# Turning the channel tiles of a Mamba block by transposing DMAs instead of by TensorE

## What is computed

```python
proj = einsum('bsd,ed->bse', xn, in_proj_w)        # gate 8192, hBC 10240, dt 128
gate, hBC, dt = split(proj)
hBC  = silu(causal_conv_of_4_taps(hBC) + conv_b)   # per channel, along the tokens
hs, Bm, Cm = split(hBC)                            # 8192 channels; 8 groups x 128; 8 x 128
dt   = clip(softplus(dt + dt_bias), 0, 100);  A = -exp(A_log)
# chunks of 128 tokens, every head h: A_cum is the running sum of dt*A in the chunk
Y_diag = (Cc @ Bc.T * exp(segsum(dt*A))) @ (hs*dt)
Y_off  = (Cc @ state) * exp(A_cum);  state = state*exp(A_cum[-1]) + Bc.T @ (hs*dt*exp(A_cum[-1]-A_cum))
y   = Y_diag + Y_off + hs*D
g   = y * silu(gate);  g = g * rsqrt(mean(g*g over 1024 channels) + 1e-5) * norm_w
out = x + g @ out_proj_w.T + base_and_lora(xn)
```

## Time and profile before

| | |
|---|---|
| median of the runs | 1740.48 us |
| the profiled execution, its own time | 1741.34 us |
| its span, first to last instruction | 1740.0 us |
| PE busy | 1676.1 us (96%) |
| DVE, ACT, POOL busy | 1377.6, 1243.3, 1069.6 us |
| mean granted clock of PE, share of full speed | 0.992 |
| DMA, share of 16 engines | 34.9% |

### The profile page before, as it was taken

How to read it: one execution, slowest core, us unless ns; L and a number is a source line. 1 busy time by engine, 2 the same in 40 slices (tenths; PEclk the granted TensorE clock), 3 DMA queues, 4 the chain that set the end, 5 groups by cost and what they waited for, 6 DMA issues and landing times.

```text
span 1740.0 us, 32221 instructions
## 1 busy us (share of the span) xinstructions
PE 1676.1 (96%) x11244; PEld 1354.9 (78%) x11244; DVE 1377.6 (79%) x1793; ACT 1243.3 (71%) x2687; POOL 1069.6 (61%) x1037
## 2 busy tenths in 40 slices
PE   6979999999999999999999999999999999999988
PEld 4667878878787878878787787878788787877766
DVE  6758788887888878887878878787787878888765
ACT  5157677776777777777777777777777777777774
POOL 3025566756677656765667566775567656775576
PEclk9989999999999999999999999999999999999999
DMA  3153243332434234332434324342343324332232
GB/s 126 62 172 101 69 140 125 135 106 77 153 120 142 89 104 143 128 125 80 140 120 140 101 80 156 116 146 90 104 138 134 126 80 139 119 135 89 86 130 95
DMA packets 97168, 202.58 MB, mean 116 GB/s; under 512 B 28392, under 2 KB 29936, under 8 KB 92784
## 3 DMA queue, kind: packets, MB, share of 16 engines
q1 hardware_dynamic: 97008, 200.51, 34.9%
HBM read 162.20 MB, written 38.28 MB: 115 GB/s over the span
## 4 chain that ended last, share of the span: by engine, by line
PE 74%; DVE 9%; ACT 8%; issue 6%; POOL 3%; DMA 1%; DVEq 0%; ACTq 0%; SPq 0%; POOLq 0%
PE P L241 22%; PE P L243 20%; PE P L242 20%; PE P L400 6%; ACT P L478 3%; PE P L287 2%; PE P L417 2%; DVE Cx L651 2%; DVE OL L882 1%; DVE hsX L651 1%; ACT GH L452 1%; POOL DL L911 1%; DVE P L861 1%; DVE hsX L657 1%; POOL GL L899 1%
## 5 line engine op out<-in xcount | busy, mean ns | idle before, releaser
L949 POOL TENSOR_TENSOR yb<-yb,dhs 128x512 f32<-128x512 f32 x112 | 144.0, 1286 | 335.8 <-DVE yb L839 335.8
L478 ACT ACTIVATE P<-AB,SC 128x128 f32<-128x128 f32 x1024 | 308.9, 372 | 0.0
L241 PE MATMUL P<-xh,AH 128*128 128x512 f32 x656 | 268.6, 409 | 9.1 <-DVE Cx L651 6.0
L651 DVE SCALAR_TENSOR_TENSOR hsX<-P,cwt,hsX 128x1023 f32<-128x1023 f32 (+2 forms) x192 | 245.6, 1279 | 16.3 <-ACT hsX L441 11.8
L243 PE MATMUL P<-xh,AL 128*128 128x512 f32 x656 | 256.9, 392 | 0.0
L242 PE MATMUL P<-xl,AH 128*128 128x512 f32 x656 | 256.5, 391 | 0.0
L241 PE MATMUL P<-GH,xh 128*128 128x512 f32 x544 | 216.9, 399 | 2.7 <-POOL GL L899 2.7
L241 PE MATMUL P<-OH,gTh 128*128 128x512 f32 x512 | 213.9, 418 | 2.3 <-issue 2.2
L243 PE MATMUL P<-GH,xl 128*128 128x512 f32 x544 | 213.5, 392 | 0.0
L242 PE MATMUL P<-GL,xh 128*128 128x512 f32 x544 | 213.0, 392 | 0.0
L894 POOL TENSOR_TENSOR AL<-AR,AH 128x512 fp32r<-128x512 f32 x82 | 107.3, 1308 | 166.2 <-ACT AH L429 166.2
(11 more groups left out here) (181 smaller groups left out, 4117.6 us busy)
## 6 DMA issues: line engine op xcount, KB each, us to landing
AB<-acr_d SPq DMA_DIRECT2D x128, 512.0 KB, 4.8
AR<-in_wa SPq DMA_DIRECT2D x80, 256.0 KB, 2.7
TS<-in_wg SPq DMA_DIRECT2D x16, 1024.0 KB, 5.3
TS<-in_wo SPq DMA_DIRECT2D x16, 1024.0 KB, 5.4
part_d<-pl SPq DMA_DIRECT2D x64, 256.0 KB, 3.1
pl<-part_d SPq DMA_DIRECT2D x64, 256.0 KB, 2.7
al<-acc_d SPq DMA_DIRECT2D x64, 256.0 KB, 3.0
acc_d<-al SPq DMA_DIRECT2D x58, 256.0 KB, 2.2
```

The lines of the kernel that those rows point to most:

```text
L241: te.matmul(o, ah_, bh_, start=(first and i == 0), stop=False)
L478: r = se.activation(E[:, h, :], AB[m % 2][:, h, :], ACT.Relu, bias=SC[s % 2][:, c, 3, h:h + 1], scale=-1.0)
L651: ve.scalar_tensor_tensor(out=o[:, d:T], in0=raw[:, 0:T - d], scalar=cwt[:, n, 3 - d:4 - d], in1=o[:, d:T], op0=ALU.mult, op1=ALU.add).the ...
L949: pe_.tensor_tensor(yb[:, :], yb[:, :], dhs[:, :], ALU.add).then_inc(s_tp, 1)
```

## The change

- Of steps 1 to 15 PE no longer turns the channel tiles (`pe_front` does so for step 0 only), ACT no longer copies them, and no bank T is taken. Instead each finished tile, a float32 array, is split into its upper and its lower 16 bits: ACT copies the upper halves (`act_high_half`), POOL the lower (`pool_low_half`), SP stores both (512 KB) in DRAM (`half_d`), and one transposing DMA per slice (`sp_turned`) reads 1024 rows of 128 two-byte items and writes them turned to `HT[m % 2]`, where high and low halves lie side by side again as float32. DVE and POOL read `HT` in SBUF. A channel tile of steps 1 to 15 lives in one of two buffers (`hsX[1][:, 0]` and `[:, 1]`) until its halves are taken.
- B and C of an even step come behind its H tiles, and every half of a projection falls one slice earlier.
- Before the loop: PE turns half of x, makes half of the dt projection, then turns the rest; the router's part of DVE's chain goes ahead of the softplus part, the reciprocal behind the LoRA product; the last channel tile of step 0 is convolved and finished in two halves of 512 tokens; the gate and the first half of the next tile stand ahead of `pe_front(0)`.

```diff
-        if s % 2 == 0:
+        if s == 0:
             tiles += [("B", s), ("C", s)]
         tiles += [("H", s, j) for j in range(4)]
+        if s and s % 2 == 0:
+            tiles += [("B", s), ("C", s)]
...
-        for c, n in enumerate((2, 1, 1, 2, 2, 1, 1, 2) if s % 2 == 0 else (0,) + (1,) * 6 + (2,) if s == 1 else (1,) * 8):
-            slot_halves[max(8 * (s - 1) + c - 1, 0)] += ks[:n]
+        for c, n in enumerate((2, 1, 1, 2, 2, 1, 1, 2) if s % 2 == 0 else (0, 0, 1, 1, 1, 1, 2, 2) if s == 1 else (1,) * 8):
+            slot_halves[max(8 * (s - 1) + c - 2, 0)] += ks[:n]
...
-            jobs += [in_turn("T", m + 1)]
+            jobs += [in_turn("T", m + 1)] if m + 1 < 8 else []
...
         def tile_out(i):
-            return Bx[:, :] if t[0] == "B" else Cx[:, :] if t[0] == "C" else hsX[t[1] % 2][:, t[2], :]
+            return Bx[:, :] if t[0] == "B" else Cx[:, :] if t[0] == "C" else hsX[t[1] > 0][:, t[2] if t[1] == 0 else t[2] % 2, :]
...
         def act_tap(i):
-            if t[0] == "H" and t[1] > 1:
-                se.wait_ge(s_t, 8 * (t[1] - 1))
+            if t[0] == "H" and t[1] and turned_no(i) > 1:
+                se.wait_ge(s_hi, turned_no(i) - 1)
+                se.wait_ge(s_lo, turned_no(i) - 1)
...
+        def act_high_half(i):
+            se.wait_ge(s_x, i + 1)
+            if n:
+                se.wait_ge(half_st[(n - 1) % 4], 16 * ((n - 1) // 4 + 1))
+            se.activation(low_high[:, 1, :], halves_of(i)[:, 1, :], ACT.Copy).then_inc(s_hi, 1)
...
         def dve_front(m):
-            o = bank("T", m)
-            ve.wait_ge(s_hsr, m + 1)
+            o = HT[m % 2]
+            if s:
+                ve.wait_ge(ht_in[m % 2], 16 * (m // 2 - 3))
+            else:
+                ve.wait_ge(s_hsr, m + 1)
...
+        def pool_low_half(i):
+            pe_.tensor_copy(low_high[:, 0, :], halves_of(i)[:, 0, :]).then_inc(s_lo, 1)
...
+        def sp_halves(i):
+            sp.wait_ge(s_hi, n + 1)
+            sp.wait_ge(s_lo, n + 1)
+            sp.dma_start(half_d[(n // 4 + 1) % 2, n % 4], low_high).then_inc(half_st[n % 4], 16)
+
+        def sp_turned(m):
+            s, c = divmod(m, 8)
+            if c == 0:
+                for j in range(4):
+                    sp.wait_ge(half_st[j], 16 * s)
+            sp.wait_ge(s_dhs, m - 1)
+            sp.wait_ge(s_xch, m - 1)
+            sp.wait_ge(s_dxh, n7(min(m - 2, 8 * ((m - 2) // 8) + 6)))
+            rows = half_d[s % 2].rearrange("j p b t -> (j p b) t")
+            sp.dma_start_transpose(HT[m % 2].bitcast(u16), rows[:, tok(c)]).then_inc(ht_in[m % 2], 16)
...
             for m in range(M + 1):
+                if m and m <= M:
+                    for k in slot_halves[m - 1]:
+                        if k % 2:
+                            sp_halves(k // 2)
+                if 8 <= m + 2 < M:
+                    sp_turned(m + 2)
                 if m >= 2:
                     sp_store(m - 2)
```

More of the change, by code:

```diff
@@ L250, in tok @@
             return slice(c * 128, (c + 1) * 128)
-        xs = [pl[0], pl[1], al[0], al[1], tg, hsr, dxh, yb]
+        xs = [pl[0], pl[1], al[0], al[1], tg, dhs, dxh, yb]
         sct_b = (xch[0], xch[1], EM[1][:, 0:512], EM[1][:, 512:1024], S, pl[0], pl[1], al[0])
@@ L304, in pe_program, with turn_x @@
         def pe_program():
-            for ti in range(NC):
+            def turn_x(ti):
                 o = bank("X", ti)
@@ L574, in act_program @@
             act_gate_hi(0)
-            for i in range(3, 6):
+            for i in range(3, 5):
                 act_tap(i)
```

191 lines of the change are left out of this document (147 added, 44 removed).

## The result

The changed kernel takes 1751.83 us (median of five runs, 1747.56 to 1755.09) against 1740.45 us of the kernel before in the same session (1739.20 to 1740.66). The ratio is 1.0065, with a 95% interval of 1.0054 to 1.0077: slower by 11 us, where 60 us less were forecast. The profiled execution took 1755.09 us, with a span of 1753.8.

A forecast was written before the change was run, and what follows sets the result against it. PE was taken to bound the kernel, issuing nearly without gaps, with DVE the candidate right behind. From 1741.3 us, −52.8 − 4.5 − 8.8 + 12.0 + 5.6 − 12.0 gave 1680.8, forecast 1680; range of 8 in 10: 1660 to 1716.

The forecast's parts named there:

- Term 1: PE's transposes in steps 1 to 15: 120 groups of 0.44 us go, all on PE's path, −52.8 us.
- Term 8: xch and dxh read SBUF: 23 to 93 us more DVE time, about what vanished hsr waits return; 0 on the path.
- Term 5: Convolutions against banks 0 and 1: their 0.36 us margin is less than the 0.44 PE gains, +5.6 us.
- Term 7: ACT's copies in the loop even out, POOL's 60 added copies are hidden by its idle time: 0, far end +15 us.
- Term 6: Before the loop: 6.5 of 8.9 us, the 1.9 us routing wait and 3.4 us of clock come back, taken as −12.
- Terms 3: BG in even steps takes an old Y's bank instead of O's, so its seven waits go: −8.8 us.
- term 4: Starts of even steps: a convolution replaces SiLU, gTl comes later, PE waits about 2.0 us at each of eight: +12.0 us.
- Term 2: Step 15: Off and St go ahead, Y starts 1.2 us earlier, 0.75 us more saved in six slices: −4.5 us.
- The second one: DVE or POOL takes the bound: collisions fall where DVE's string has no slack, 1708 us (1698 to 1725); chance 0.20.
- three signs by which the prediction would be wrong: DVE's front waits for DMAs past a step's first slice; xch plus dxh exceed 2.5 us; PE's loop waits exceed 50.
- The rival on the slow side: Slow transposing DMA: DVE's front and POOL's dhs wait at HT, 1900 us at 10 us per transfer; chance 0.11.

The follow-up runs named there:

- Experiment 1: Kernel before, with PE turning only one of the four 128x128 pieces of each tile in steps 1 to 15: 1725.05 us, ratio 0.9913.
- experiment 5: Changed kernel, with DVE's xch and dxh on 5 of 8 heads in steps 1 to 15: 1723.14 us, ratio 0.9917.
- experiment 2: Kernel before, with DVE's xch and dxh reading the turned tile from ACT's copy in SBUF instead of bank T in PSUM: 1752.19 us, ratio 1.0069.
- experiments 3: Changed kernel, with ACT copying the DMA-turned tile into bank T in PSUM, where xch and dxh read it: 1762.24 us, ratio 1.0125.
- experiment 8: Kernel before, with only tiles B and C of even steps put behind the four H tiles of their step: 1739.34 us, ratio 0.9997.
- experiment 7: Changed kernel, with POOL's copy of the low halves cut from 1024 to 8 items per partition: 1733.18 us, ratio 0.9960.
- all reliefs: Changed kernel, with xch and dxh on 5 of 8 heads, POOL's low-half copy cut to 8 items, and Off ahead of the projection: 1729.90 us, ratio 0.9941.

## Why the prediction was wrong

**Term 1** was right in what PE loses (52.6 us measured, 52.8 forecast) and wrong in what follows from it. Here the prediction failed: it took the 52.8 us to be "all on PE's path". It had said itself that a saving counts only "unless another engine is right behind". One was, and I had its row: 0.36 us of room before the convolution's bank. Experiment 1 puts the share that reaches the end at 15 of 40 us.

**Term 8**, "I take 0 on the path", is the second failed step. The two operations took 86 us more, inside the stated 23 to 93, and this was not hidden: taking 57 us off DVE was worth 29 us (experiment 5), and adding 58 us of such reads to the kernel before cost 12 (experiment 2). I had balanced it against the 87.7 us of waits on `hsr`. That is a balance of sums over the run, and says nothing of the single pass.

**Term 5** allowed 5.6 us more for the convolutions' bank. Measured are 26.3 us, with those on B, against 8.0: 18 more. Neither cheaper reads (experiments 3 and 5) nor the tile order (experiment 8) account for them, and less work on PE alone brought 6.6 (experiment 1). And one wait has no term at all: O's bank, which `yb` frees, 16.4 us in 20 waits and none before. Of these, 8.5 us lie in six slices of step 15, seven waits of 0.4 us lie in passes where SiLU stands ahead of `yb`, and seven of 0.7 us in passes where it does not. I had followed only the waits that the profile of before shows.

**Term 7** took 0 for POOL's copy, with 15 as the far end; leaving it out gave 19 (experiment 7), collisions included.

**Term 6**: the wait of 8.9 us went, as said. That of 1.9 us on the routing did not (1.8 us, at the same 44 us), a new one of 3.0 us for POOL's `DL` came at 125 us, and the 3.4 us of clock did not come: from 40 to 60 us the granted clock is 0.83 in both kernels. The first gated result is turned at 132.2 us instead of 136.9, so 4.7 of the 12 us came; step 0 then lost 1.6 of them.

**The clock** is no term of the sum but for the 3.4 us of term 6. It cost the 15 us of doubled distances counted above. The changed kernel's own five runs say the same: 1747.56 us at 0.989, 1749.02 at 0.986, 1753.11 at 0.984, 1751.83 at 0.983, 1755.09 at 0.981, about 0.9 us for each thousandth, while the kernel before stayed at 0.992 to 0.994.

**Terms 3 and 4.** BG's wait (8.8 us) is gone. The wait of St behind `gTl` at the starts of even steps came as computed, 2.2 us against 2.0, in seven starts where term 4 counted eight, with 0.6 for Gt behind it that I had not seen.

**Term 2** was right about Y and missed the next wait. In a slice of step 15 Y starts 1.2 us earlier behind the turning, as forecast (2.06 us against 3.31 in the earlier trace rows), and then O waits for `yb` to free Off's bank:

```profile
1692.54 0.60 PE L453 MATMUL P<-ident,yb 128*128 128x128 f32 x4
...
1694.60 1.15 PE L436 MATMUL P<-xch,EM 128*64 128x64 f32 x32
1697.53 0.50 PE L250 MATMUL P<-OH,gTh 128*128 128x512 f32 x1 [1.77 <-DVE yb L952]
```

From the last turning of step 14 to the last of step 15 it took 81.4 us, before 78.8. The dearer reads are part of it: the kernel before takes 81.2 us there with them (experiment 2), and the changed one 78.3 when they are cut (experiment 5).

**The rivals.** The second one, DVE taking the bound, is what happened, and it was sized at +28 over the forecast where +72 came. It contained the convolution's waits, but not O's bank, nor the clock. Of the three signs by which the prediction would be wrong, one came: PE's waits from 135 us on add up to 78 us, over the 50 (35 in the kernel before). The other two did not: `xch` and `dxh` take 2.1 us together in the mean, and DVE waits for no transposing DMA. The rival on the slow side was a slow DMA, and the transfer landed in 3.8 us, though its rows of 256 bytes are twice as long as the pieces of SC that the prediction called equal; the one that should have stood there was this same mechanism at its full price.

How far the account goes, as an estimate from the runs: 1681 us of the forecast, 33 more since experiment 1 gives term 1 some 20 us instead of 53, 4.5 more since term 2 did not come, and 7 more since term 6 gave 4.7 instead of 12, make 1726 us. The changed kernel with all reliefs took 1729.9. The other 22 us, up to 1751.8, are what the reliefs of DVE, POOL and PE's order gave together. That it meets so closely may be luck, as the parts of the sum are not independent.

What stays open: why the three reliefs don't add up, where the waits for convolutions beyond those of experiment 1 come from (the projection's halves also fall one slice earlier, which no run tests), and how much is the clock. No kernel here holds the clock and changes only the waits.

## What to carry to other kernels

A gapless engine is not necessarily the only bound: before counting what is taken off it, look at how far ahead of it the engine that feeds it finishes, slice by slice, and count a saving in full only where that distance is larger. Then ask which wait ends last once an instruction starts earlier; the profile of before cannot show it. Sums over the run of a cost and a gain on one engine don't show that they cancel. Leave the filler (here SiLU) where its engine waits anyway.

## What the runs showed of the hardware

- A DVE product of 128x512 with both inputs in SBUF takes 675 ns at least, 684 to 693 in the median and up to 1809 ns; in the row above, of 1.79 us, its end follows that of a POOL instruction.
- Behind waits of 2.2 and 0.6 us in a row PE ran at 1.2 GHz for some 6 us. The clock fell behind six of seven such pairs of waits, and behind three of seven single waits of 1.9 us.
- A transposing DMA of 256 KB with 16-bit items lands in 3.8 us (median of 120) and takes SP's queue 1.2 us to issue (least 1159, median 1222, most 2350 ns; SP's other transfers 0.3 to 0.6 us in the median). The queue's share rose from 34.9 to 50.8% for 63 MB more, 284 us of 16 engines instead of the 189 that I had put at 3.0 us per MB.
